# Routed expert rows scattered to both choices' places by the fused stage, and the two expert passes joined into one stream that adds into the output

## The chip, the cores and the metric

The kernel runs on one core of one Trainium2 chip. The metric is the time on the device in microseconds. Three runs of the kernel before gave 1041.34, 1044.93 and 1046.5 us; the median is 1044.93 us.

## The reference, cut to what matters

The input x has 32 batches of 256 tokens of 256 features (8192 tokens), float32. A gated cross-attention comes first; then every token goes through a shared gated MLP and through two of 16 experts:

```
x = x + tanh(g_xattn) * xattn(layernorm(x), ctx, ...)
xf = layernorm(x).reshape(-1, 256)
scores = softmax(xf @ Wg.T);  wk, idx = top_k(scores, 2)
cw = sum(one_hot(idx, 16) * wk)
h = gated_mlp_act(xf @ W1[e])                    # 256 -> 2*128 -> 128, for each expert
z = sum over e of cw[t, e] * (h @ W2[e])
x = x + tanh(g_ffn) * (z + gated_mlp_act(xf @ Ws1) @ Ws2)
```

The change touches only how the rows of the tokens reach their experts, and how the two experts' results are added.

## The kernel before

The kernel has four stages, one after the other: a preparation, the attention (batch by batch, until about 540 us of the profiled span), the fused stage `mix` (until about 752 us) and the expert stage `passes` (until the end).

**mix.** It goes through the 8192 tokens in 16 steps G of 512 tokens. A step holds its tokens in one of NX = 5 buffers `row[G % NX]`, 128 partitions x 4 x ROW with ROW = 516: columns 0 to 255 are the running sum (x1, to which the shared MLP's result is added), 256 to 511 the normalised token y, and the last four are the tail: the token's number, its place (slot) for the first choice, and the two weights. For each step TensorE transposes y, scores the experts, does the shared MLP (`hidden`, `down`) and counts places (`rank`); VectorE chooses the two experts (`choose`), writes the places (`place`, L1172) and the weights (`weigh`, L1159) and adds the MLP's result (`add_x1`, L1199, which counts up `added`). GpSimd's program for a step is: `note(G)` (the token numbers, L942), `low_weights(G)` (the low half of expert G's weights, L947, which waits for ScalarE's high half, L1073), then `scatter(G - 1)`: four indirect DMAs of 128 rows each (L956) that put whole 2064-byte rows into `rows1_scratch`, at the place for the second choice. SyncE loads the rows of step G + 3 (L887) when the scatter of step G - 2 has freed their buffer, and the weights; after the last step it writes blank rows behind each expert's last row (`blank_tails`, 16 DMAs, L1286).

**passes.** Each pass takes 80 tiles of 128 rows, which belong to one expert each, as 40 pairs. The first pass reads `rows1_scratch`, computes the second choice's expert, adds the result to the running sum in the row and scatters the whole 2064-byte row to the first choice's place in `rows0_scratch` (L1364). The second pass reads `rows0_scratch`, adds the first choice's expert and scatters 1024-byte rows to the output (L1364 again). For pair q:

- SyncE (`load`, L1335) waits until buffer `row[q % U]`, U = 10, has been scattered, loads two row numbers (L1341) and issues two DMAs (L1344).
- TensorE does `transpose_rows(q)` (L1386, 4 transposes), `hidden(q - 1)` (12 products into ps_h), `transpose_a(q - 2)` (L1407) and `down(q - 3)` (6 products into ps_z). These products are recorded under the lines of the helper `products`, L75 to L77.
- ScalarE copies the high halves (L1457, L1467) and does the silu (L1462); VectorE makes the low halves (L1482, L1495), multiplies (L1489), and adds ps_z to the row (L1500), which counts up `final`.
- GpSimd (`send`, L1359) waits for `final`, and issues two indirect DMAs.

After the loads of pair q == U SyncE writes all 16 blank tails of `rows0_scratch`. Between the passes it waits for every scatter of the first pass (L1352), since the second pass reads what they wrote. TensorE, ScalarE and VectorE run each pass as 10 written-out pairs, a hardware loop over three further rounds of 10, and a drain; GpSimd runs a loop over 4 rounds in each pass.

Of the kernel before, what the change touches and what calls it, by code (L numbers as in the profile page):

```python
# [28 lines left out]
P = 128  # L29
# [425 lines left out]
def attend(nc, c, a):  # L455


    with ExitStack() as ctx:
# [45 lines left out]
        with nc.Block() as block:  # L504

            @block.sync
            def _(sp):
# [6 lines left out]
                def blank_rows(dram):  # L514

                    sp.dma_start(dram[SLOT_ROWS:ROWS, :], c.blank[:, :]).then_inc(c.blanked, 16)
# [19 lines left out]
                blank_rows(c.rows1)  # L536
                blank_rows(c.rows0)
# [258 lines left out]
def mix(nc, c):  # L796
# [6 lines left out]
    with ExitStack() as ctx:  # L803
# [52 lines left out]
        l_done, masked, gap_ready, tanh_done = sem("l_done"), sem("masked"), sem("gap_ready"), sem("tanh_done2")  # L856
        ranked, counted, placed, chain = sem("ranked"), sem("counted"), sem("placed"), sem("chain")
# [15 lines left out]
        with nc.Block() as block:  # L873

            @block.sync
            def _(sp):
# [30 lines left out]
                blank_tails(nc, sp, nc.sync, c, c.rows1, 1, range(E), c.blanked1)  # L907

            @block.gpsimd
            def _(pool):  # L910
# [29 lines left out]
                def note(G):  # L940
                    wait(pool, scattered[G % NX], 64 * (G // NX))
                    g.tensor_copy(tail_of(G)[:, :, 0].bitcast(I32), tokens[:, 4 * G:4 * G + 4]).then_inc(noted, 1)  # L942
# [22 lines left out]
                for u in range(NX):  # L965
                    pool.wait_ge(scattered[u], 64 * len(range(u, STEPS, NX)))
# [147 lines left out]
            def _(v):  # L1114
# [44 lines left out]
                def weigh(G):  # L1159
# [10 lines left out]
                    V.tensor_tensor(tail[:, :, 3], over[:, :, E], tail[:, :, 2], ALU.mult)  # L1170

                def place(G):  # L1172
                    wait(v, scattered[G % NX], 64 * (G // NX))
# [103 lines left out]
def blank_tails(nc, eng, queue, c, dram, choice, experts, done):  # L1277


    for first in experts[::4]:  # L1280
        with ExitStack() as registers:
            held = [registers.enter_context(eng.register(f"tail_{choice}_{first + i}")) for i in range(4)]
            eng.load(held, c.tails[0:1, choice * E + first:choice * E + first + 4])
            for register in held:
                at = eng.snap(register, donate=True, min_val=0, max_val=SLOT_ROWS - P)
                queue.dma_start(dram[bass.ds(at, P), :], c.blank[:, :]).then_inc(done, 16)  # L1286


def passes(nc, c):


    U = 10
    ROUNDS = PAIRS // U
    YROW, META_AT = D, 2 * D
    with ExitStack() as ctx:
# [13 lines left out]
        go = sem("send_go")  # L1309
# [5 lines left out]
        def rounds(eng, step, first, lag=0):  # L1315


            last = first + ROUNDS
            for u in range(U):
                step(U * first + u, u, first)  # L1320
            with eng.Fori(first + 1, last) as j:
                for u in range(U):
                    step(U * j + u, u, j)
            for u in range(lag):
                step(U * last + u, u, last)

        def inside(first):

            return lambda q: not isinstance(q, int) or U * first <= q < U * (first + ROUNDS)

        with nc.Block() as block:

            @block.sync
            def _(sp):
                def load(dram, q):  # L1335
                    u = q % U
                    wait(sp, scattered[u], 32 * (q // U))
                    with ExitStack() as registers:
                        held = [registers.enter_context(sp.register(f"rows_{q}_{i}")) for i in range(2)]
                        first = 2 * q  # L1340
                        sp.load(held, c.rows_at[0:1, first:first + 2])  # L1341
# [9 lines left out]
                for u in range(U):  # L1351
                    sp.wait_ge(scattered[u], 32 * ROUNDS)  # L1352
                sp.wait_ge(c.blanked0, 16 * E)
                for q in range(PAIRS, 2 * PAIRS):
                    load(c.rows0, q)

            @block.gpsimd
            def _(pool):
                def send(q, u, dram, columns, index, bound):  # L1359
                    pool.wait_ge(final, q + 1)  # L1360
                    pool.sem_inc(go, 1)
                    for i in range(2):
                        target = row[u][:, i, META_AT + index:META_AT + index + 1].bitcast(I32)
# [4 lines left out]
                with pool.Fori(0, ROUNDS) as j:  # L1368
                    for u in range(U):
                        send(U * j + u, u, c.rows0, ROW, 1, SLOT_ROWS - 1)  # L1370
                with pool.Fori(ROUNDS, 2 * ROUNDS) as j:
                    for u in range(U):
                        send(U * j + u, u, c.out, D, 0, T - 1)
                for u in range(U):
                    pool.wait_ge(scattered[u], 64 * ROUNDS)

            @block.tensor
            def _(pe):


                def transpose_rows(q, u, j):
                    pe.wait_ge(row_in[u], 32 * (j + 1))
                    wait(pe, yT_lo, q - 1)
                    for i in range(2):
                        for k in range(DC):
                            last = nc.tensor.transpose(ps_y[u % 2][:, k, i * P:(i + 1) * P],  # L1386
                                                       row[u][:, i, YROW + k * P:YROW + (k + 1) * P], c.ident[:, :])
# [6 lines left out]
                def hidden(q, p, at):  # L1394
                    pe.wait_ge(yT_lo, q + 1)
                    wait(pe, a_done, 2 * (q - 1))
                    for i in range(2):
                        token = slice(i * P, (i + 1) * P)
                        last = products(nc, ps_h[p][:, i, :], [
                            (yT[p][0][:, k, token], yT[p][1][:, k, token], *split(at[i], k * D)) for k in range(DC)])  # L1400
                    last.then_inc(h_done, 1)

                def transpose_a(q, p):
                    pe.wait_ge(a_done, 2 * q + 2)
                    wait(pe, aT_lo, q - 1)
                    for i in range(2):
                        last = nc.tensor.transpose(ps_a[p][:, i, :], a[p][:, i, :], c.ident[:, :])  # L1407
                    last.then_inc(aT_done, 1)

                def down(q, p, at):  # L1410
                    pe.wait_ge(aT_lo, q + 1)
                    wait(pe, final, q - 1)
                    for i in range(2):
                        last = products(nc, ps_z[p][:, i, :], [
                            (aT[p][0][:, i, :], aT[p][1][:, i, :], *split(at[i], DC * D))])
                    last.then_inc(z_done, 1)

                def load_weights_at(known, q, u):


                    _, at = nc.values_load_multi_w_load_instructions(
                        c.weights_at[0:1, bass.ds(2 * q + 2, 4)], engines=[mybir.EngineType.PE], min_val=0,
                        max_val=(E - 1) * WROW, skip_runtime_bounds_check_because="the table is made of min(., E - 1)")
                    known[u], known[u + 1] = at[0:2], at[2:4]

                for first in (0, ROUNDS):
                    exists, known = inside(first), {}

                    def step(s, u, j):
                        if u == 0:  # L1430
                            known.clear()
                            if exists(s - 3):
                                load_weights_at(known, s - 3, -3)
                        if u % 2 == 0:
                            load_weights_at(known, s - 1, u - 1)
                        if exists(s):
                            transpose_rows(s, u, j)
# [148 lines left out]
```

## Time and profile before

| | us |
|---|---|
| median of the runs | 1044.93 |
| the profiled execution | 1043.86 |
| its span in the trace | 1041.7 |
| TensorE busy | 909.5 (87%) |
| VectorE busy | 804.5 (77%) |
| ScalarE busy | 478.8 (46%) |
| GpSimd busy | 475.1 (46%) |

All times below are from the start of this span. 2.2 us of the execution's own time lie outside it. Busy time is that of recorded instructions; an engine that waits, or issues DMAs, isn't counted as busy. PE is TensorE, PEld its weight loads, DVE VectorE, ACT ScalarE, POOL GpSimd, SPq and POOLq the sequencers of SyncE and GpSimd.

### The profile page before, as it was taken

To read this page: it belongs to the slowest core of one execution; us is meant where nothing else is said; L and a number is where in the kernel's file an instruction comes from. 1 tells how busy PE (TensorE), PEld (TensorE's weight loads), DVE (VectorE), ACT (ScalarE), POOL (GpSimd) and SP (SyncE) were. 2 spreads that over 40 slices of the span, in tenths; PEclk is the share of its full clock that TensorE was granted. 3 is DMA by queue.
4 is the path that set the end of the run, shared out by engine and by line. 5 is a ranking of instruction groups with operands and counts; after the bars stand their busy time and mean duration, and the time that the engine had idled before them with its cause. 6 is when DMAs were issued, how large, how long until landed. Compare 5 with 4: busy or idle time off the path is not lost. (4 is left out here: it accounts for less than half of the span.)

```text
span 1041.7 us, 22369 instructions
## 1 busy us (share of the span) xinstructions
PE 909.5 (87%) x6728; PEld 857.2 (82%) x6729; DVE 804.5 (77%) x1837; ACT 478.8 (46%) x970; POOL 475.1 (46%) x495
## 2 busy tenths in 40 slices
PE   2559999999999999999949999999565899599994
PEld 2449999999999999998847888887465899499994
DVE  5768888888898888998737898888534677467773
ACT  3345555555555555554445455543122344144441
POOL 6134434343343434334321555455415466537775
PEclk9999999999999999999968999999868899889998
DMA  8621222122221222212151444442769899488890
GB/s 216 215 87 35 80 68 67 54 57 79 66 79 45 66 66 67 68 54 67 53 172 32 173 166 160 170 170 108 275 222 318 284 341 344 146 267 260 268 289 29
DMA packets 108096, 150.64 MB, mean 145 GB/s; under 512 B 21622, under 2 KB 72186, under 8 KB 108032
## 3 DMA queue, kind: packets, MB, share of 16 engines
q1 hardware_dynamic: 92672, 107.60, 34.1%
q0 software_dynamic: 15360, 42.24, 10.6%
q8 instruction: 35, 0.57, 0.2%
q14 instruction: 29, 0.24, 0.1%
HBM read 90.19 MB, written 65.90 MB: 150 GB/s over the span
## 5 line engine op out<-in xcount | busy, mean ns | idle before, releaser
L549 POOL TENSOR_TENSOR prob<-prob,row_sum 128x616 f32<-128x616 f32 x64 | 77.9, 1218 | 148.7 <-DVE row_sum L739 148.7
L1364 POOL DMA_INDIRECT rows_scratch<-prow x80 | 78.7, 983 | 75.0 <-DVE prow L1500 47.2
L956 POOL DMA_INDIRECT rows_scratch<-row,slot x64 | 67.8, 1060 | 75.8 <-DVE row L1203 61.2
L1364 POOL DMA_INDIRECT out<-prow x80 | 78.7, 983 | 50.1 <-issue 26.4
L1482 DVE TENSOR_TENSOR eyT_lo<-ps_ey,eyT_hi 128x512 fp32r<-128x512 f32 x80 | 55.2, 690 | 55.6 <-ACT eyT_hi L1457 55.1
L1457 ACT ACTIVATE eyT_hi<-ps_ey 128x512 fp32r<-128x512 f32 x80 | 47.9, 599 | 109.3 <-PE ps_ey L1386 109.3
L75 PE MATMUL ps_h<-w_flat,eyT_hi 128*128 x320 | 98.1, 307 | 0.0
L224 POOL TENSOR_TENSOR xT_lo<-xT_raw,xT_hi 128x512 fp32r<-128x512 f32 x32 | 41.2, 1286 | 121.7 <-ACT ctxb_hi L190 121.6
L1386 PE MATMUL ps_ey<-ident,prow 128*128 128x128 f32 x320 | 51.6, 286 | 49.2 <-DMA prow<-rows_scratch 45.9
L190 ACT ACTIVATE M_hi<-ps_proj 128x308 f32 (+1 forms) x128 | 54.4, 429 | 84.1 <-PE ps_proj L77 84.0
L76 PE MATMUL ps_h<-w_flat,eyT_hi 128*128 x320 | 90.9, 284 | 0.0
L77 PE MATMUL ps_h<-w_flat,eyT_lo 128*128 x320 | 90.7, 283 | 0.0
L75 PE MATMUL ps_s<-M_hi,xT_hi 128*128 (+1 forms) x256 | 81.4, 318 | 8.7 <-PEq L315 8.5
L1489 DVE SCALAR_TENSOR_TENSOR a<-ps_h,prow,silu 128x128 f32<-128x128 f32 x160 | 48.8, 347 | 47.8 <-ACT silu L1462 47.8
L195 DVE TENSOR_TENSOR PT_lo<-ps_pt,PT_hi 77x512 fp32r<-77x512 f32 x128 | 80.9, 671 | 0.3 <-ACT PT_hi L190 0.3
L1386 PEld LDWEIGHTS ps_ey<-ident,prow 128*128 128x128 f32 x320 | 38.5, 147 | 51.7 <-DMA prow<-rows_scratch 47.3
L76 PE MATMUL ps_s<-M_lo,xT_hi 128*128 (+1 forms) x256 | 78.6, 307 | 0.0
L77 PE MATMUL ps_s<-M_hi,xT_lo 128*128 (+1 forms) x256 | 78.6, 307 | 0.0
L75 PE MATMUL ps_o<-wo_hi,OT_hi 128*128 128x256 f32 x256 | 74.6, 291 | 1.4 <-DVE OT_lo L195 1.4
L75 PE MATMUL ps_o<-PT_hi,V_hi 96*128 96x256 f32 x256 | 72.9, 285 | 3.3 <-DVE PT_lo L195 3.3
L675 ACT ACTIVATE prob<-prob,rstd 128x616 f32<-128x616 f32 x64 | 52.0, 812 | 44.8 <-DVE prob L729 44.8
L76 PE MATMUL ps_o<-PT_lo,V_hi 96*128 96x256 f32 x256 | 72.4, 283 | 0.0
(232 smaller groups left out, 3383.3 us busy)
## 6 DMA issues: line engine op xcount, KB each, us to landing
prow<-rows_scratch SPq DMA_DIRECT2D x160, 258.0 KB, 3.8
rows_scratch<-blank SPq DMA_DIRECT2D x34, 258.0 KB, 4.0
xs<-in_x SPq DMA_DIRECT2D x16, 512.0 KB, 4.5
xT_raw<-in_xT SPq DMA_DIRECT2D x32, 256.0 KB, 3.8
x_tok<-in_x SPq DMA_DIRECT2D x32, 256.0 KB, 2.9
x_scratch<-x_tok SPq DMA_DIRECT2D x32, 256.0 KB, 3.0
row<-x_scratch SPq DMA_DIRECT2D x16, 512.0 KB, 4.0
w_raw<-in_W SPq DMA_DIRECT2D x16, 256.0 KB, 3.5
```

The lines of the kernel that those rows point to most:

```text
L75: nc.tensor.matmul(out, lh, rh, start=start and n == 0, stop=False)
L76: nc.tensor.matmul(out, lh, rl, start=False, stop=False)
L77: last = nc.tensor.matmul(out, ll, rh, start=False, stop=stop and n == len(pairs) - 1)
L190: nc.scalar.activation(out, source, ACT.Copy).then_inc(done, 1)
L195: nc.vector.tensor_tensor(lo, source, f32(hi), ALU.subtract).then_inc(done, 1)
L549: nc.gpsimd.tensor_tensor(pr, pr, row_sum[i][:, :].unsqueeze(2).broadcast_to((P, H, CK)), ALU.mult).then_inc(normed, 1)
L675: nc.scalar.activation(prob[i][:, :], prob[i][:, :], ACT.Exp, scale=c.rstd1[:, bass.ds(2 * b + i, 1)]).then_inc(exp_done, 1)
L956: pool.indirect_dma_start(c.rows1, bass.IndirectOffsetOnAxis(slot1[:, t:t + 1], 0), row[G % NX][:, i, :], None).then_inc(scattered[G % NX] ...
L1364: pool.indirect_dma_start(dram, bass.IndirectOffsetOnAxis(target, 0), row[u][:, i, 0:columns], None, bounds_check=bound, oob_is_err=False) ...
L1386: last = nc.tensor.transpose(ps_y[u % 2][:, k, i * P:(i + 1) * P], row[u][:, i, YROW + k * P:YROW + (k + 1) * P], c.ident[:, :])
L1482: V.tensor_tensor(yT[p][1][:, :, :], ps_y[p][:, :, :], f32(yT[p][0][:, :, :]), ALU.subtract).then_inc(yT_lo, 1)
L1489: V.scalar_tensor_tensor(a[p][:, i, :], ps_h[p][:, i, 0:HID], row[b][:, i, weight:weight + 1], silu[p][:, i, :], ALU.mult, ALU.mult).then_ ...
```

## The change

The fused stage now scatters each row to both choices' places. `rows1_scratch` gets the whole row as before; `rows0_scratch` has rows of 260 floats (1040 bytes: y and the tail), and gets four further indirect DMAs for each step, issued ahead of the four old ones once `weigh` has counted up a new semaphore `weighed`. A buffer is free after 128 instead of 64 counts (each DMA counts 16).

In the expert stage the first pass scatters its 1024-byte sums to the output, and the second pass, which loads only 1040-byte rows, adds to the output with an indirect DMA that has `compute_op=add`. VectorE's last operation of a pair is a copy in the second pass instead of an addition. SyncE no longer waits between the passes; GpSimd waits there, once, until the first pass's scatters have landed. The blank tails of `rows0_scratch` are half as large and are written in four groups of four. U is 13 instead of 10, and all engines' programs are written out for 80 pairs, without loops. The core of the diff:

```diff
                 def load_rows(G):
                     u = G % NX
-                    wait(sp, scattered[u], 64 * (G // NX))
+                    wait(sp, scattered[u], 128 * (G // NX))
...
                 def scatter(G):
                     pool.wait_ge(noted, G + 1)
+                    pool.wait_ge(weighed, G + 1)
+                    for i in range(4):
+                        slot0 = row[G % NX][:, i, 2 * D + 1:2 * D + 2].bitcast(I32)
+                        pool.indirect_dma_start(c.rows0, bass.IndirectOffsetOnAxis(slot0, 0),
+                                                row[G % NX][:, i, D:], None).then_inc(scattered[G % NX], 16)
                     for i in range(4):
                         if i % 2 == 0:
                             pool.wait_ge(added, 2 * G + i // 2 + 1)
...
-                    V.tensor_tensor(tail[:, :, 3], over[:, :, E], tail[:, :, 2], ALU.mult)
+                    V.tensor_tensor(tail[:, :, 3], over[:, :, E], tail[:, :, 2], ALU.mult).then_inc(weighed, 1)
...
-    U = 10
-    ROUNDS = PAIRS // U
+    U = 13
+    LAST = 2 * PAIRS
...
                         for i in range(2):
                             at = sp.snap(held[i], donate=True, min_val=0, max_val=ROWS - P)
-                            sp.dma_start(row[u][:, i, :], dram[bass.ds(at, P), :]).then_inc(row_in[u], 16)
+                            if q < PAIRS:
+                                sp.dma_start(row[u][:, i, :], c.rows1[bass.ds(at, P), :]).then_inc(row_in[u], 16)
+                            else:
+                                sp.dma_start(row[u][:, i, D:], c.rows0[bass.ds(at, P), :]).then_inc(row_in[u], 16)
                 sp.wait_ge(c.blanked1, 16 * E)
                 for q in range(PAIRS):
-                    load(c.rows1, q)
-                    if q == U:
-                        blank_tails(nc, sp, nc.sync, c, c.rows0, 0, range(E), c.blanked0)
-                for u in range(U):
-                    sp.wait_ge(scattered[u], 32 * ROUNDS)
+                    load(q)
+                    first = (q - U) * 4 // 6
+                    if q >= U and (q - U) % 6 == 0 and first < E:
+                        blank_tails(nc, sp, nc.sync, c, c.rows0, 0, range(first, first + 4), c.blanked0, c.blank[:, D:])
                 sp.wait_ge(c.blanked0, 16 * E)
-                for q in range(PAIRS, 2 * PAIRS):
-                    load(c.rows0, q)
+                for q in range(PAIRS, LAST):
+                    load(q)
...
-                def send(q, u, dram, columns, index, bound):
+                def send(q, op):
                     pool.wait_ge(final, q + 1)
-                    pool.sem_inc(go, 1)
                     for i in range(2):
-                        target = row[u][:, i, META_AT + index:META_AT + index + 1].bitcast(I32)
+                        token = row[q % U][:, i, META_AT:META_AT + 1].bitcast(I32)
                         pool.indirect_dma_start(
-                            dram, bass.IndirectOffsetOnAxis(target, 0), row[u][:, i, 0:columns], None,
-                            bounds_check=bound, oob_is_err=False).then_inc(scattered[u], 16)
+                            c.out, bass.IndirectOffsetOnAxis(token, 0), row[q % U][:, i, 0:D], None, bounds_check=T - 1,
+                            oob_is_err=False, compute_op=op).then_inc(scattered[q % U], 16)
...
+                for q in range(PAIRS):
+                    send(q, ALU.bypass)
                 for u in range(U):
-                    pool.wait_ge(scattered[u], 64 * ROUNDS)
+                    pool.wait_ge(scattered[u], 32 * len(range(u, PAIRS, U)))
+                for q in range(PAIRS, LAST):
+                    send(q, ALU.add)
...
-                            V.tensor_tensor(row[b][:, :, 0:D], ps_z[p][:, :, :], row[b][:, :, 0:D],
+                        if q < PAIRS:
+                            V.tensor_tensor(row[q % U][:, :, 0:D], ps_z[q % 2][:, :, :], row[q % U][:, :, 0:D],
                                             ALU.add).then_inc(final, 1)
+                        else:
+                            V.tensor_copy(row[q % U][:, :, 0:D], ps_z[q % 2][:, :, :]).then_inc(final, 1)
```

## Rows read from the trace of the kernel before

**Rows 1.** Page, part 2: busy tenths in 40 slices of the span.
```profile
PE   2559999999999999999949999999565899599994
...
DMA  8621222122221222212151444442769899488890
```

**Rows 2.** Timeline of TensorE: start, us, instruction, idle before it.
```profile
764.20 1.11 PE L1386 MATMUL ps_ey<-ident,prow 128*128 128x128 f32 x4 [17.19 <-DMA prow<-rows_scratch]
...
810.46 1.12 PE L1386 MATMUL ps_ey<-ident,prow 128*128 128x128 f32 x4 [14.15 <-DMA prow<-rows_scratch]
...
837.75 0.63 PE L1386 MATMUL ps_ey<-ident,prow 128*128 128x128 f32 x4 [1.05 <-issue]
```

**Rows 3.** Stretches: us, busy by engine, clock, DMA share, GB/s.
```profile
577.00:697.00 120.00, 117.25 (x818) 102.94 (x817) 107.62 (x341) 60.98 (x123) 63.77 (x61) 1.00 0.47 167
...
840.00:895.00 55.00, 54.16 (x473) 53.99 (x473) 42.96 (x99) 24.43 (x59) 37.84 (x39) 1.00 0.94 328
...
925.00:1020.00 95.00, 94.57 (x825) 94.05 (x824) 74.96 (x172) 43.25 (x104) 67.52 (x69) 1.00 0.81 254
```

**Rows 4.** Timeline of VectorE: the last operation of a pair.
```profile
776.30 0.68 DVE L1500 TENSOR_TENSOR prow<-ps_z,prow 128x512 f32<-128x512 f32 x1
...
787.26 0.68 DVE L1500 TENSOR_TENSOR prow<-ps_z,prow 128x512 f32<-128x512 f32 x1
...
898.95 0.69 DVE L1500 TENSOR_TENSOR prow<-ps_z,prow 128x512 f32<-128x512 f32 x1 [0.35 <-PE ps_z L77]
...
923.35 0.68 DVE L1500 TENSOR_TENSOR prow<-ps_z,prow 128x512 f32<-128x512 f32 x1
...
1023.21 0.68 DVE L1500 TENSOR_TENSOR prow<-ps_z,prow 128x512 f32<-128x512 f32 x1
...
1027.74 0.69 DVE L1500 TENSOR_TENSOR prow<-ps_z,prow 128x512 f32<-128x512 f32 x1 [0.25 <-PE ps_z L77]
```

**Rows 5.** Line L956: time from its DMAs' issue to landing.
```profile
DMA to landing us min/median/max: 2.7/3.0/7.7
```

**Rows 6.** Timeline of SyncE's queue, 760 to 885 us.
```profile
760.70 23.33 SPq L1344 DMA_DIRECT2D prow<-rows_scratch  x22
784.54 17.83 SPq L1286 DMA_DIRECT2D rows_scratch<-blank  x16
```

**Rows 7.** Groups of GpSimd, 577.4 to 696.9 us (ten steps).
```profile
L956 POOL DMA_INDIRECT rows_scratch<-row,slot x40 | 43.2, 1080 | 47.6 <-DVE row L1203 38.5 <-issue 9.1
...
L942 POOL COPY row<-tokens 128x4 int32<-128x4 int32 x10 | 2.0, 203 | 0.0
```

**Rows 8.** Timeline of GpSimd in the fused stage.
```profile
565.18 1.84 POOL L947 TENSOR_TENSOR w_flat<-w_raw,w_flat 128x768 fp32r<-128x768 f32 x1 [14.57 <-ACT w_flat L1073]
...
637.20 1.85 POOL L947 TENSOR_TENSOR w_flat<-w_raw,w_flat 128x768 fp32r<-128x768 f32 x1 [0.82 <-ACT w_flat L1073]
...
646.75 1.38 POOL L956 DMA_INDIRECT rows_scratch<-row,slot  x1 [0.30 <-issue]
...
649.14 1.85 POOL L947 TENSOR_TENSOR w_flat<-w_raw,w_flat 128x768 fp32r<-128x768 f32 x1 [0.81 <-ACT w_flat L1073]
654.84 1.00 POOL L956 DMA_INDIRECT rows_scratch<-row,slot  x1 [3.85 <-DVE row L1203]
...
751.37 0.97 POOL L956 DMA_INDIRECT rows_scratch<-row,slot  x1 [0.30 <-issue]
```

**Rows 9.** Timeline of GpSimd at the end.
```profile
1024.76 0.98 POOL L1364 DMA_INDIRECT out<-prow  x1 [0.47 <-issue]
...
1033.78 0.98 POOL L1364 DMA_INDIRECT out<-prow  x1 [0.30 <-issue]
```

**Rows 10.** Page, part 3: DMA queues, packets, MB, share of 16 engines.
```profile
q1 hardware_dynamic: 92672, 107.60, 34.1%
q0 software_dynamic: 15360, 42.24, 10.6%
```

More of the change, by code:

```diff
@@ L906, in _ @@
                 sp.wait_ge(tails_ready, 1)
-                blank_tails(nc, sp, nc.sync, c, c.rows1, 1, range(E), c.blanked1)
+                blank_tails(nc, sp, nc.sync, c, c.rows1, 1, range(E), c.blanked1,
+                            c.blank[:, :])
             @block.gpsimd
@@ L965, in _ @@
                 for u in range(NX):
[L966 removed]
+                    pool.wait_ge(scattered[u], 128 * len(range(u, STEPS, NX)))
             @block.tensor
@@ L1274, in _, with blank_tails @@
                 V.tensor_copy(c.rows_at[:, :], ps_table[:, CHOICES * SLOT_TILES:])
-def blank_tails(nc, eng, queue, c, dram, choice, experts, done):
+def blank_tails(nc, eng, queue, c, dram, choice, experts, done, source):
     for first in experts[::4]:
         with ExitStack() as registers:
-            held = [registers.enter_context(eng.register(f"tail_{choice}_{first + i}")) for i in range(4)]
+            held = [registers.enter_context(eng.register(f"tail_{done.name}_{first + i}")) for i in range(4)]
             eng.load(held, c.tails[0:1, choice * E + first:choice * E + first + 4])
@@ L1313, in passes @@
             sem("aT_done"), sem("aT_hi"), sem("aT_lo"), sem("z_done"), sem("final"))
-        def rounds(eng, step, first, lag=0):
-            last = first + ROUNDS
-            for u in range(U):
[L1320 to L1329, printed above, removed]
         with nc.Block() as block:
@@ L1334, in _, with load @@
             def _(sp):
-                def load(dram, q):
+                def load(q):
                     u = q % U
@@ L1413, in down @@
                     for i in range(2):
-                        last = products(nc, ps_z[p][:, i, :], [
-                            (aT[p][0][:, i, :], aT[p][1][:, i, :], *split(at[i], DC * D))])
+                        last = products(nc, ps_z[q % 2][:, i, :], [
+                            (aT[q % 2][0][:, i, :], aT[q % 2][1][:, i, :], *split(at[i], DC * D))])
                     last.then_inc(z_done, 1)
[L1418 to L1437, printed above, removed]
-                        if exists(s - 1):
-                            hidden(s - 1, (u - 1) % 2, known[u - 1])
-                        if exists(s - 2):
-                            transpose_a(s - 2, u % 2)
-                        if exists(s - 3):
-                            down(s - 3, (u - 3) % 2, known[u - 3])
-                    rounds(pe, step, first, lag=3)
+                known = {}
@@ new lines, in _ @@
+                for s in range(LAST + 3):
+                    q = s - 1
+                    if 0 <= q < LAST and q % 2 == 0:
+                        registers = ExitStack()
+                        held = [registers.enter_context(pe.register(f"weights_{q}_{i}")) for i in range(4)]
+                        pe.load(held, c.weights_at[0:1, 2 * q + 2:2 * q + 6])
+                        at = [pe.snap(r, donate=True, min_val=0, max_val=(E - 1) * WROW) for r in held]
+                        known[q], known[q + 1] = (at[0:2], None), (at[2:4], registers)
+                    if s < LAST:
+                        transpose_rows(s)
+                    if 0 <= s - 1 < LAST:
+                        hidden(s - 1, known[s - 1][0])
+                    if 0 <= s - 2 < LAST:
+                        transpose_a(s - 2)
+                    if s >= 3:
+                        at, registers = known.pop(s - 3)
+                        down(s - 3, at)
+                        if registers:
+                            registers.close()
```

136 lines of the change are left out of this document (63 added, 73 removed).

## The prediction

> **What bounds the kernel now.** I read the busy slices first [rows 1]. TensorE is at nine tenths in most of the attention and the fused stage, and falls in three places of the last third, where the DMA row doesn't fall but mostly rises. The timeline of TensorE shows what two of them are [rows 2]: transposes of an expert pair that wait for loaded rows, 17.19 us ahead of the first pair and 14.15 us at 810. The third is the stop between the passes. Everywhere else the expert stage is bound by TensorE: from 840 to 895 us it is busy 54.16 of 55.00 us, from 925 to 1020 94.57 of 95.00, at a granted clock of 1.00, which is the 2.4 GHz level [rows 3]. A pair takes (787.26 - 776.30) / 4 = 2.74 us [rows 4]; over ten pairs it is 2.745, which I use. The fused stage is bound by TensorE too (117.25 of 120.00 us), while GpSimd has room: 63.77 of 120.00 [rows 3].
>
> **The expert stage.** From the first pair's last operation to the 80th's the trace has 1027.74 - 776.30 = 251.4 us [rows 4]. A stream at TensorE's pace takes 76 intervals of 2.745 us, 208.6 us, and for the last three, when no further pair is started, the 1027.74 - 1023.21 = 4.5 us seen now: 213.1 us. The difference of 38.3 us is what the change can take out here. It has three parts.
>
> - The stop between the passes: 923.35 - 898.95 = 24.4 us between two pairs [rows 4], in which the first pass drains, its scatters land and the loads begin anew. One interval of 2.7 us stays, and a pass that drains is quicker by 8.2 - 4.5 = 3.7 us, which the joined stream has once and not twice: 18.0 us go. Pass two no longer reads what pass one writes, so nothing on SyncE or TensorE waits there. The wait is GpSimd's alone, about 3 us from issue to landing [rows 5].
> - The stop at 810 with the slow matmuls behind it: SyncE spent 17.83 us on 16 blank DMAs between the loads of two pairs [rows 6], with ten buffers to live on. Now a group of four costs SyncE at most 4 x 17.83 / 16 = 4.5 us and writes half the bytes, and six pairs' loads (12 x 23.33 / 22 = 12.7 us) go with it: 17.2 us against six pairs of TensorE, 16.5 us. That is nearly even, and three more buffers give 8.2 us of distance. I cost the blanks at nothing; what hides them is that distance, and without it each group would cost its 4.5 us. About 17 us go.
> - The loops' ends: 1.05 us of idle TensorE at 837.75 [rows 2] and shorter ones at the other ends; the rest of the 38.3, about 3 us. Written-out code has no jump there. Should its code arrive late beside the busy DMA queues, at six places such a stop would cost 6 us; should it not, nothing. I take nothing, as 54.16 of 55.00 us hold one loop's end and no other stop.
>
> The DMAs have room. Pass one moved 328 GB/s at a share of 0.94; now it reads the same and writes half, which is what pass two does at present, at 254 GB/s and 0.81 [rows 3]. VectorE's last operation becomes a copy from the same PSUM tile, between nothing and its 0.68 us shorter; VectorE is busy 74.96 of 95 us and the path gets nothing of it. The weights' register loads are the same, one for two pairs.
>
> **The price in the fused stage.** GpSimd issues four more indirect DMAs for each of 16 steps. A group of four takes 4.32 us and 0.91 us of gaps now, 5.23 us [rows 7]; the four new ones, at 0.97 and 0.30 each, 5.1 us. The weights' low half is 1.85 us [rows 8], the copy 0.20 [rows 7], the gap behind them 0.3. That is 12.7 us of work for a step that now takes 649.14 - 637.20 = 11.94 us. GpSimd waits 3.85 us for `added` and 0.81 us for ScalarE's high half in it [rows 8], 4.7 us together, and these go first; what is over makes GpSimd this stage's bound. From its low_weights at 565.18 on it doesn't wait again: 567.0 + 0.3 + 16 x (5.23 + 5.10) + 14 x (0.20 + 1.85 + 0.30) = 765.5 us for its last scatter, instead of 751.37 + 0.97 = 752.3 [rows 8]. That is 13.2 us later. Queued behind the late scatters on GpSimd are `note` and `low_weights`, for which SyncE's loads of weights wait; for the scatters themselves SyncE's reload of the buffer waits, and for that ScalarE. Five buffers absorb the first steps' lateness, then TensorE gets small waits; these are the same lateness and don't add to it. The expert stage's first load waits for the last scatter, so all of it is on the path. The duration doesn't go by bytes: a 2064-byte row and a 1024-byte row give 0.97 and 0.98 us [rows 8, 9]. From both sides: if all 64 new ones were like the long one at 646.75, 1.38 us [rows 8], it would be 26 us more; if all new ones hid in the two waits, 13.2 less. I take the row that three of four show.
>
> **The adding DMA.** No row shows one. The nearest is the plain one: 0.98 us and a gap of 0.30, two for a pair, 2.56 us, 0.18 below TensorE's pair [rows 9]. A lower bound is the same 0.98 us (it must do all that the plain one does). For the upper one I count that an adding DMA moves a row three times (out of the buffer, out of the output, back) and a plain one twice: 0.98 x 3 / 2 = 1.47 us. At 0.98 pass two stays TensorE's, and GpSimd's wait of 3 us between the passes is made up in 17 pairs. GpSimd decides from (2.745 - 0.60) / 2 = 1.07 us on. Then from pair 40 it needs 3 us and 40 pairs of its own, where TensorE's pace ends after 36 x 2.745 + 4 x 2.56 = 109.1 us. At 1.47: 3 + 40 x 3.54 = 144.6, 35.5 us more. Rows of any kind cost GpSimd the same, so I stay near the plain row, a quarter of the way: 1.10 us, 3 + 40 x 2.80 = 115.0, 5.9 us more.
>
> The trace's indirect DMA takes 0.97 us for 128 rows of either length [rows 8, 9]. By the Trainium skill (Collectives: The Full Stack, "The bandwidth ceiling: the fold count and why AG ≠ RS ≠ AR") a reduce emits two read descriptors for each chunk where a copy emits one; if GpSimd's time went by descriptors, the sum would get the 35.5 us. By the same skill (DMA: Bandwidth & Descriptors, "Anatomy of one DMA") descriptor generation is a small part, and the sum would get nothing. No row here decides between them; the first is rival 2.
>
> The end is as before: 14.0 us from the last pair's operation to the span's end, in which GpSimd issues its last DMAs until 1034.8 [rows 4, 9].
>
> **The sum.** -38.3 + 13.2 + 5.9 = -19.2 us. From the profiled execution's own 1043.86 us that is 1024.7; it lay 1.1 us under the median of 1044.93, and against that I say 1025.7 us.
>
> **Rivals.**
>
> 1. Adding costs GpSimd nothing: -25.1 us, 1019.8. For it: the duration has no regard to bytes. Against: the second read must be described somewhere.
> 2. Adding costs GpSimd 1.47 us: -25.1 + 35.5 = +10.4, 1055, slower. It decides from 1.34 us on, where the gain is gone. For it: 128 rows in 0.98 us leave 8 ns for a row, which looks like work for each row. Pass two would have pairs of 3.54 us, ended by buffers that come free late.
> 3. The DMA engines can't add fast enough. The software queue moved 42.24 MB in 10.6% of 16 x 1041.7 us, 23.9 GB/s an engine, the hardware queue 18.9 [rows 10]. A pair of pass two loads 266 KB, 14.1 us of engine time, and adds 8192 / 40 rows of 1 KB, 8.8 us if plain; 16 engines have 43.9 us in a pair. The engines decide when an adding row costs 3.4 plain ones. At 4.5 a pair is 3.36 us: +24.5 us, 1044, the same. Against: 0.81 is the share now [rows 3].
> 4. GpSimd pays more in the fused stage, since it now always runs beside VectorE: 1 us more for a step, 16 us, 1041.7, the same. For it: the 1.38 us row; against: the other three of four.
> 5. The new scatters hide in GpSimd's idle half: -13.2, 1012.5. Against: its waits are 4.7 us of a step, its new work 5.1 and 0.3 more.
> 6. The blanks still starve TensorE, once by half of the old stop: +7, 1033. Against: 13 buffers.
>
> **The numbers.** Forecast, 1021.5 to 1034 with rival 6 in it: 0.42. Rival 1, 1018 to 1021.5: 0.22. Rival 5: 0.06. Rivals 3 and 4, 1034 to 1048: 0.17. Rival 2: 0.13. The likeliest cases' own range is 1018 to 1034. The range of 1013 to 1048 leaves out rival 2 and a part of rival 5, under 2 in 10. A measurement of this kernel can tell 0.5%, 5.2 us, from no change. Faster (below 1039.7): 0.42 + 0.22 + 0.06 and half of rivals 3 and 4, 0.78. Within 0.5%: 0.10, with the earliest of rival 2. Slower (above 1050.2): 0.12.
>
> **What would show it.** In the fused stage GpSimd almost without idle and steps of 12.7 us; its last scatter near 765; TensorE with small waits in the later steps. In the expert stage an unbroken row of nines, pairs of 2.745 us, and no wait of TensorE for rows except ahead of the first pair. GpSimd's adding DMA near 1.10 us. The prediction is wrong if that DMA is far above 1.1 us (pairs over 2.8 us, and finished pairs queued at the end), if transposes wait for rows in pass two while GpSimd waits too (slow adding), if the stream stops with the releaser "issue", or if the fused stage's steps stay at 11.95 us.

## The result: 1063.25 us, slower by 1.7%

The changed kernel took 1063.25 us in the median of four runs (1062.11 to 1064.02), the kernel before, beside it, 1045.11 us. The ratio is 1.0171 (95% interval 1.0148 to 1.0195). I had forecast 1025.7 us, a range of 1013 to 1048, and "slower" at 0.12: wrong in its direction, and outside the range.

The page of the changed kernel first: the busy slices, to be held against [rows 1], and one line of the groups.

```profile
PE   2659999999999999999849999998479999998840
...
POOL 5133434344443434344135888888616667788886
...
L1356 POOL DMA_INDIRECT out<-prow x160 | 203.6, 1273 | 85.6 <-issue 51.3
```

The three holes in TensorE's row have become one, as forecast. But its nines end early, and in the last slices, where TensorE has nothing to do, GpSimd goes on. Its 160 scatters of the expert stage have a mean of 1273 ns, and a mean over two forms hides both. GpSimd's timeline shows them: plain ones up to 902 us, the wait between the passes, then adding ones to the end.

```profile
902.18 0.99 POOL L1356 DMA_INDIRECT out<-prow  x1 [0.31 <-DMA out<-prow]
907.04 1.58 POOL L1356 DMA_INDIRECT out<-prow  x1 [3.88 <-DMA out<-prow]
908.93 1.59 POOL L1356 DMA_INDIRECT out<-prow  x1 [0.30 <-issue]
910.83 1.56 POOL L1356 DMA_INDIRECT out<-prow  x1 [0.30 <-issue]
...
1052.44 1.56 POOL L1356 DMA_INDIRECT out<-prow  x1 [0.30 <-issue]
1054.31 1.56 POOL L1356 DMA_INDIRECT out<-prow  x1 [0.30 <-issue]
```

An adding DMA takes 1.56 us and a gap of 0.30, so a pair costs GpSimd 3.72 us, and 40 pairs from 907.04 us on give 1055.8, where its last one ends. VectorE finished the last pair's rows long before. Its timeline shows the last operation of pairs 40 and 41, the first two of pass two when pairs are counted from 0, and of the last pair, 79:

```profile
902.22 0.68 DVE L1482 COPY prow<-ps_z 128x512 f32<-128x512 f32 x1
905.03 0.68 DVE L1482 COPY prow<-ps_z 128x512 f32<-128x512 f32 x1
...
1024.58 0.69 DVE L1482 COPY prow<-ps_z 128x512 f32<-128x512 f32 x1 [0.35 <-PE ps_z L77]
```

From its end at 1025.3 us on GpSimd works alone for 30.6 us, and the span ends 6.4 us later. How the lateness builds up stands in the windows (us, busy by engine PE, PEld, DVE, ACT, POOL with counts, clock, DMA share, GB/s):

```profile
577.00:697.00 120.00, 112.50 (x785) 98.84 (x783) 108.11 (x323) 59.88 (x119) 98.34 (x96) 1.00 0.56 198
840.00:895.00 55.00, 55.00 (x471) 54.94 (x470) 43.78 (x99) 24.50 (x58) 38.08 (x39) 1.00 0.81 257
900.00:920.00 20.00, 20.00 (x173) 20.00 (x172) 15.88 (x37) 8.91 (x22) 13.27 (x10) 1.00 0.57 98
920.00:940.00 20.00, 20.00 (x172) 19.97 (x172) 15.87 (x36) 8.80 (x21) 16.83 (x11) 1.00 0.82 138
940.00:1020.00 80.00, 68.07 (x545) 65.03 (x544) 50.20 (x115) 28.32 (x68) 66.89 (x44) 0.98 0.82 132
1040.00:1062.00 22.00, 0.00 (x0) 0.00 (x0) 0.00 (x0) 0.00 (x0) 13.43 (x9) 0.50 0.05 3
```

TensorE is full until 940 us, and by VectorE's timeline pairs go on at 2.81 us until 955: thirteen buffers and the rows already loaded let it run on at its own pace while unsent pairs pile up. Only then do the buffers run out, and it waits for rows whose load waits for GpSimd. GpSimd's 66.89 of 80 us is 44 x 1.56 minus the window's edges: the rest is the 0.30 us gap behind each, so it isn't idle at all. TensorE's small waits and the last 31 us are one and the same lateness. The waits of 795 to 1040 us name the rows, not their cause (us in total, times, longest):

```profile
POOL out L1356 <- issue: 47.8, 130, 0.6
...
PE ps_ey L1378 <- DMA prow<-rows_scratch: 11.7, 13, 2.7
```

The blanks starve nothing: TensorE waits 0.9 us for rows between its first transposes and 940 us. SyncE's queue (start, us spent issuing) answers to [rows 6]:

```profile
773.21 24.82 SPq L1336 DMA_DIRECT2D prow<-rows_scratch  x28
798.78 1.99 SPq L1295 DMA_DIRECT2D rows_scratch<-blank  x4
802.28 12.17 SPq L1336 DMA_DIRECT2D prow<-rows_scratch  x12
814.96 3.10 SPq L1295 DMA_DIRECT2D rows_scratch<-blank  x4
```

Between the two kernels' spans, 1041.7 and 1062.3 us, the 20.6 us divide so:

| stretch | before | after | difference |
|---|---|---|---|
| start to the expert stage's first load | 760.70 | 773.21 | +12.5 |
| to the first pair's last operation | 15.6 | 14.9 | -0.7 |
| to pair 40's (first of pass two) | 147.1 | 114.1 | -33.0 |
| to the end of the span | 118.3 | 160.1 | +41.7 |

### The profile page after: what moved, and what is told of

Read it like the earlier page. It is cut to its first block and busy times, and to the rows that moved or that the text cites. A ratio compares the mean times of both kernels' runs of the same rounds, so it can differ in the third digit from the quotient of the medians.

```text
span 1062.3 us, 21947 instructions
## 1 busy us (share of the span) xinstructions
PE 912.8 (86%) x6728; PEld 859.3 (81%) x6728; DVE 815.3 (77%) x1837; ACT 479.0 (45%) x970; POOL 583.6 (55%) x559
## 5 line engine op out<-in xcount | busy, mean ns | idle before, releaser
L1356 POOL DMA_INDIRECT out<-prow x160 | 203.6, 1273 | 85.6 <-issue 51.3
L965 POOL DMA_INDIRECT rows_scratch<-row,slot x64 | 67.5, 1055 | 19.5 <-issue 15.5
L77 PE MATMUL ps_o<-PT_hi,V_lo 96*128 96x256 f32 x256 | 73.0, 285 | 0.0
L959 POOL DMA_INDIRECT rows_scratch<-row x64 | 62.8, 981 | 17.5 <-issue 17.5
```

The costliest lines, as they stand in the source:

```text
L77: last = nc.tensor.matmul(out, ll, rh, start=False, stop=stop and n == len(pairs) - 1)
L959: pool.indirect_dma_start(c.rows0, bass.IndirectOffsetOnAxis(slot0, 0), row[G % NX][:, i, D:], None).then_inc(scattered[G % NX], 16)
L965: pool.indirect_dma_start(c.rows1, bass.IndirectOffsetOnAxis(slot1[:, t:t + 1], 0), row[G % NX][:, i, :], None).then_inc(scattered[G % NX] ...
L1356: pool.indirect_dma_start(c.out, bass.IndirectOffsetOnAxis(token, 0), row[q % U][:, i, 0:D], None, bounds_check=T - 1, oob_is_err=False, c ...
```

## The experiments

Thirteen runs follow, of eleven kernels. Each kernel is an edit of the changed one, but for two that edit the kernel before. A ratio is to the kernel before as it ran beside the kernel of the experiment, on the same chip; its median was 1043.71 or 1044.35 us.

**The second pass without adding.**

```diff
                 for q in range(PAIRS, LAST):
-                    send(q, ALU.add)
+                    send(q, ALU.bypass)
```

> The changed kernel, but the second pass's scatter writes instead of adding (the output then holds only the first choice's part). Theory A: the adding DMA's 1.56 us on GpSimd is all that makes pass two slow. Then each of its DMAs takes 0.98 us, pairs are 2.81 us as in pass one, and the execution loses about 41 us: near 1022. Rival: pass two would be slow anyway, from the doubled use of the output or from loads of 1040-byte rows; then pairs stay above 2.9 us and the time above 1030.

It took 1019.88 us (1018.76 to 1023.0), 0.9775 of the kernel before (0.974 to 0.981). Rival 1 had said 1019.8. All 160 scatters are alike now, and GpSimd's idle time is back (its groups from 785 us on):

```profile
L1356 POOL DMA_INDIRECT out<-prow x160 | 157.4, 984 | 90.0 <-issue 60.8 <-DVE prow L1479 24.5 <-DVE prow L1482 2.4
```

Behind the first pair TensorE waits for rows nowhere in the stream. The word "add" alone costs 1063.25 - 1019.88 = 43.4 us between the two medians. The two did not run side by side; by their ratios to the kernel before it is 1.0171 - 0.9775, some 41 us, and from pair 40 to the end of the span the traces have 160.1 us with it and 1019.2 - 899.2 = 120.0 without. So it is 40 to 43 us. With its measured 1.56 us my own formula gives 3 + 40 x 3.72 - 109.1 = 42.7. Everything else in the change is worth 24 us of gain, where the prediction had 25.1.

**Without the new scatters of the fused stage.** The second pass reads the columns y and tail of the first pass's rows; the waits go back to 64 counts.

```diff
-                    for i in range(4):
-                        slot0 = row[G % NX][:, i, 2 * D + 1:2 * D + 2].bitcast(I32)
-                        pool.indirect_dma_start(c.rows0, bass.IndirectOffsetOnAxis(slot0, 0),
-                                                row[G % NX][:, i, D:], None).then_inc(scattered[G % NX], 16)
...
-                                sp.dma_start(row[u][:, i, D:], c.rows0[bass.ds(at, P), :]).then_inc(row_in[u], 16)
+                                sp.dma_start(row[u][:, i, D:], c.rows1[bass.ds(at, P), D:]).then_inc(row_in[u], 16)
```

> The changed kernel, but the fused stage scatters only to rows1 (four DMAs for each step), and pass two reads the y and tail columns of rows1 at pass one's places, so that its values are wrong while its amount of work is the same. Theory A: the four further DMAs make the fused stage end later by their lateness on GpSimd, 13 to 14 us, and nothing else: near 1050, with the expert stage as in the changed kernel. Rival: they are hidden, and the later start comes from elsewhere: 1060 or more.

It took 1053.08 us (1049.29 to 1054.14), 10.2 less than the changed kernel; its first load comes at 759.90 instead of 773.21 us, 13.3 earlier. Of these 13.3 us, 4.5 were there before the fused stage's new scatters began (GpSimd's low weights just ahead of them start at 563.89 and 568.42 us), which leaves 8.8. GpSimd has its idle time of the fused stage again, as in [rows 7] (577 to 697 us):

```profile
L961 POOL DMA_INDIRECT rows_scratch<-row,slot x40 | 43.2, 1081 | 47.9 <-DVE row L1208 38.8 <-issue 9.1
```

So the step of the prediction that put the new scatters on the path holds, at 9 to 10 us instead of its 13.2. The price of adding outweighs the gain by itself: this kernel adds and has no new scatters, and is still slower than the kernel before (1.0093; 1.0064 to 1.0123). The price of the new scatters alone doesn't: the kernel of the experiment above pays it and is faster.

**Fewer rows for each scatter.** The passes' scatters send 64 or 16 of the 128 rows of a tile.

```diff
-                        token = row[q % U][:, i, META_AT:META_AT + 1].bitcast(I32)
+                        token = row[q % U][0:64, i, META_AT:META_AT + 1].bitcast(I32)
...
-                            c.out, bass.IndirectOffsetOnAxis(token, 0), row[q % U][:, i, 0:D], None, bounds_check=T - 1,
+                            c.out, bass.IndirectOffsetOnAxis(token, 0), row[q % U][0:64, i, 0:D], None, bounds_check=T - 1,
```

> The changed kernel, but both passes' indirect DMAs send only the first 64 of each tile's 128 rows (half of the output is missing). Theory A: GpSimd's time goes by the descriptions it writes, two for a plain row and three for an adding one. Then both durations fall, by rows: the plain one from 0.98 to 0.5 to 0.75 us, the adding one from 1.56 to 0.8 to 1.1, and the step between them halves from 0.58 to about 0.29 us. Rival B, a dearer fixed set-up for an adding DMA: the step stays at 0.58. Rival C, GpSimd is held back by the DMA engines that add: the adding one falls to the plain one's duration, since the engines then have half the work.

> The changed kernel, but both passes' indirect DMAs send only the first 16 of each tile's 128 rows (most of the output is missing). With 64 rows the durations were 0.91 and 1.41 us, with 128 they are 0.98 and 1.56. Theory B, a fixed set-up, dearer for an adding DMA, and a small part for each row: along that line 0.86 and 1.29 us. Theory A, all of it for rows, is left only if the durations now fall far below 0.8 and 1.2.

One run each: 1050.65 us with 64 rows, 1035.15 us with 16. With 64 rows, one plain DMA of GpSimd's timeline and the group of the second pass (915 to 1000 us); then the groups of both passes with 16 (870 to 895 and 915 to 985 us):

```profile
879.48 0.91 POOL L1356 DMA_INDIRECT out<-prow  x1 [0.30 <-issue]
...
L1356 POOL DMA_INDIRECT out<-prow x50 | 70.1, 1402 | 15.2 <-issue 13.4 <-DVE prow L1482 1.8
```

```profile
L1356 POOL DMA_INDIRECT out<-prow x19 | 16.0, 841 | 10.5 <-DVE prow L1479 7.4 <-issue 3.0
...
L1356 POOL DMA_INDIRECT out<-prow x45 | 57.5, 1278 | 13.7 <-issue 12.2 <-DVE prow L1482 1.5
```

| rows | plain, us | adding, us | difference |
|---|---|---|---|
| 16 | 0.84 | 1.28 | 0.44 |
| 64 | 0.91 | 1.40 | 0.49 |
| 128 | 0.98 | 1.56 | 0.58 |

A line through each column: plain 0.82 us and 1.3 ns for a row, adding 1.24 us and 2.5 ns. Of the 0.58 us, 0.42 is there however few rows are sent, and 0.16 goes by rows. A theory in which adding merely doubles the work for each row explains the second part, not the first. Why the fixed part is dearer no run shows. Even with 16 rows an adding DMA and its gap take 1.28 + 0.30 = 1.58 us, above the 2.745 / 2 = 1.37 us at which GpSimd begins to decide.

**A quarter of the bytes.** The scatters send 64 of the 256 columns.

```diff
-                            c.out, bass.IndirectOffsetOnAxis(token, 0), row[q % U][:, i, 0:D], None, bounds_check=T - 1,
+                            c.out.rearrange("t (k d) -> (t k) d", d=64), bass.IndirectOffsetOnAxis(token, 0), row[q % U][:, i, 0:64], None, bounds_check=T - 1,
```

> The changed kernel, but both passes' indirect DMAs send only the first 64 of a row's 256 columns, to rows of 256 bytes (most of the output is missing). Theory: GpSimd's time has nothing to do with bytes; the durations stay at 0.98 and 1.56 us, the pairs of pass two at 3.72 us and the time at about 1063. Rival: the adding DMAs are slow at the DMA engines and hold GpSimd back; then the 1.56 falls to 1.2 or less with a quarter of the bytes.

This kernel ran once, on a chip on which the kernel before took 1106.27 us, so its own 1109.86 us can't be set against the others; the duration on GpSimd can. All 160 together, and the last ones by the timeline:

```profile
L1356 POOL DMA_INDIRECT out<-prow x160 | 203.5, 1272 | 119.3 <-DVE prow L1479 74.3
```

```profile
1098.33 1.56 POOL L1356 DMA_INDIRECT out<-prow  x1 [0.30 <-issue]
1100.19 1.56 POOL L1356 DMA_INDIRECT out<-prow  x1 [0.30 <-issue]
```

The mean is within 1 ns of that with four times the bytes. Together with the run of 16 rows, where an eighth of the rows still takes 1.28 of the 1.56 us, it says that the cost is GpSimd's in issuing, not the transfer's, and rival 3 (the DMA engines) has nothing left to stand on.

**The blanks of the kernel before, moved.** Two kernels with the old design. In the first the 16 blank tails of `rows0_scratch` are issued at the end of the fused stage, in the second behind the first pass's last load.

```diff
                 blank_tails(nc, sp, nc.sync, c, c.rows1, 1, range(E), c.blanked1)
+                blank_tails(nc, sp, nc.sync, c, c.rows0, 0, range(E), c.blanked0)
```

```diff
                     load(c.rows1, q)
-                    if q == U:
-                        blank_tails(nc, sp, nc.sync, c, c.rows0, 0, range(E), c.blanked0)
+                blank_tails(nc, sp, nc.sync, c, c.rows0, 0, range(E), c.blanked0)
```

> The kernel before, but SyncE writes the blank tails of rows0 at the end of the fused stage, where it waits, instead of between the loads of pass one. If the stop at 810 us came from these 16 DMAs alone, it goes: 14 to 17 us less, near 1029. If the ring of ten buffers is too short for DMA queues at 0.94 of their time, part of it stays as waits for rows: 1035 to 1040.

> The kernel before, but SyncE writes the 16 blank tails of rows0 after the last load of pass one, where its queue waits for the drain. They are then beside scatters alone and must land before the wait for the last scatter is over. If so, the stop at 810 goes and the expert stage's start stays where it was: 15 to 17 us less, 1028 to 1030. If the blanks are still in flight at the pass's end, the stop between the passes grows by up to 6 us: 1034.

The early ones gave 1034.2 us (1031.65 to 1034.63), a ratio of 0.9901 (0.987 to 0.9932); the late ones 1030.09 us (1026.38 to 1032.89), 0.9873 (0.9836 to 0.9911). Both lose the stop at 810 us. The late ones came out as expected, the early ones 5 us slower than hoped: there the blanks delay the first load instead, from 760.70 to 768.08 us (SyncE's queue):

```profile
735.47 27.71 SPq L1287 DMA_DIRECT2D rows_scratch<-blank  x32
768.08 30.94 SPq L1345 DMA_DIRECT2D prow<-rows_scratch  x26
```

Late, they lie in the stop between the passes, which is there anyway, while the first pass drains (SyncE's queue until 960 us):

```profile
867.61 17.99 SPq L1286 DMA_DIRECT2D rows_scratch<-blank  x16
891.54 68.73 SPq L1344 DMA_DIRECT2D prow<-rows_scratch  x54
```

That is a gain of 14 us for one call moved out of a loop, behind its end. Of the kernels here that compute the whole, it is the fastest: below the kernel before and below the changed one.

**The joined stream without an adding DMA.** The first pass scatters its sums by the first choice's place into a scratch of their own, and the second loads them with SyncE, four pairs ahead, and adds on VectorE; eleven buffers.

```diff
+                def load_sums(q):
+                    u = q % U
...
+                            sp.dma_start(row[u][:, i, 0:D], c.sums0[bass.ds(at, P), :]).then_inc(sum_in[q % 4], 16)
...
+                for q in range(PAIRS, LAST):
+                    if q >= PAIRS + 4:
+                        sp.wait_ge(final, q - 3)
+                    load_sums(q)
+                    if q + 7 < LAST:
+                        load(q + 7)
```

> A joined stream without an adding DMA: the fused stage scatters as in the changed kernel; pass one writes its sums with the plain indirect DMA to a scratch by the first choice's places; pass two loads y and the tail early and the sums by a DMA of SyncE's, four pairs ahead of their use, once pass one's scatters have landed; VectorE adds them as before. 11 buffers. GpSimd then has 2.56 us for a pair in both passes. Between the passes VectorE's last operation waits for the first sums, some 5 to 9 us instead of a stop of 18. Expected 1022 to 1030: the 1020 of the writing second pass and that wait. Rival: the third and fourth load of a pair on SyncE's queue, or the DMA engines, make pass two slower than 2.81 us: 1035 or more.

1055.54 us (1053.71 to 1057.12), a ratio of 1.0106 (1.0082 to 1.0129): a miss, by the rival that was named. GpSimd is relieved, and the wait sits on VectorE (its groups, 905 to 1050 us, and SyncE's queue at 940 us):

```profile
L1498 DVE TENSOR_TENSOR prow<-ps_z,prow 128x512 f32<-128x512 f32 x41 | 28.3, 690 | 50.4 <-DMA prow<-sums_scratch 47.6 <-PE ps_z L77 2.3 <-issue 0.4
```

```profile
940.51 0.87 SPq L1355 DMA_DIRECT2D prow<-sums_scratch  x2
942.11 1.09 SPq L1340 DMA_DIRECT2D prow<-rows_scratch  x2
943.90 0.85 SPq L1355 DMA_DIRECT2D prow<-sums_scratch  x2
```

Two DMAs take SyncE mostly 0.85 us, but with the two row numbers for them a group starts only every 1.5 to 1.8 us, and a pair has two such groups: 3.1 to 3.6 us, over the 2.8 us that a pair takes where TensorE decides. From its first load of sums at 910.55 to 1050 us SyncE waits only once, for 0.2 us. The queue that was relieved at the boundary became the bound. From pair 40 to the last pair it takes 127.7 us, the kernel without adding 105.9: 22 us more. Up to pair 40 it takes 12.5 us more, at the boundary for the most part, where I had expected 5 to 9.

**Ten buffers.** Pairs in the changed kernel take 2.81 us, not 2.745. Theory: the written-out code. Rival: the thirteen buffers.

```diff
-    U = 13
+    U = 10
...
-                    send(q, ALU.add)
+                    send(q, ALU.bypass)
```

> The changed kernel with ten buffers instead of 13, and a writing instead of an adding second scatter (the output then holds only the first choice's part). Pairs take 2.81 us in the changed kernel's pass one and 2.74 before. Theory: written-out code costs it; then pairs stay at 2.81. Rival: the 13 buffers moved the other tiles in memory, or the deeper ring does it: then 2.74, and some 5 us less than with 13. If ten buffers are too few for four blanks between loads, TensorE shows waits for rows, some us in all.

One run, 1016.57 us. The last operations of its first pairs:

```profile
787.75 0.68 DVE L1479 TENSOR_TENSOR prow<-ps_z,prow 128x512 f32<-128x512 f32 x1
...
790.50 0.68 DVE L1479 TENSOR_TENSOR prow<-ps_z,prow 128x512 f32<-128x512 f32 x1
...
793.24 0.68 DVE L1479 TENSOR_TENSOR prow<-ps_z,prow 128x512 f32<-128x512 f32 x1
```

2.745 us again, in written-out code; the code isn't it. The buffers make the difference, by their number or by where the tiles behind them come to lie. I tried to tell these apart with a pad of 32 bytes behind thirteen and behind ten buffers, each kernel run twice.

```diff
         row = [sb(f"prow{i}", [P, 2, ROW]) for i in range(U)]
+        sb("pad", [P, 8])
```

> As e1 (13 buffers, a writing second scatter, the output holds only the first choice's part), with 32 unused bytes in each partition behind the buffers. 13 buffers of 4128 bytes end 32 bytes off a multiple of 64, 11 do too (pairs of 2.80 us), 10 don't (2.745). Theory: the tiles behind them lie badly for TensorE's reads, and with the 32 bytes pairs take 2.745 us again, 5 us less than e1 in all. Rival: the number of buffers itself does it; pairs stay at 2.81.

> As e5 (ten buffers, a writing second scatter, the output holds only the first choice's part), with the 32 unused bytes behind the buffers, which move the tiles behind them off the multiple of 64. Theory: pairs of 2.81 us instead of 2.745, about 5 us more than e5's 1016.6. Rival: no change.

> e9 again: 13 buffers with 32 unused bytes behind them, a writing second scatter. Theory of the tiles' place: pairs of 2.745 us, the time near 1015. Rival, the number of buffers: 2.81 us, 1020.

> e12 again: ten buffers with 32 unused bytes behind them, a writing second scatter. Theory of the tiles' place: pairs of 2.81 us. Rival: 2.745 us.

The four ran on two chips on which the kernel before takes 1106.27 and 1104.79 us: 1110.28 and 1118.23 us with thirteen, 1102.67 and 1116.42 with ten. There pairs of 2.1 and 5 us alternate in either kernel, which buries a difference of 0.065 us in the times of pairs.

Within a pair the traces say a little more. Most of the extra time, 0.05 to 0.06 of the 0.065 us, lies in the twelve products of `hidden`, which TensorE starts one after the other. Their second and their twelfth, with ten buffers, and with ten buffers and the pad (TensorE's timelines):

```profile
852.55 0.28 PE L76 MATMUL ps_h<-w_flat,eyT_hi 128*128 x1
...
853.70 0.28 PE L77 MATMUL ps_h<-w_flat,eyT_lo 128*128 x1
```

```profile
854.17 0.29 PE L76 MATMUL ps_h<-w_flat,eyT_hi 128*128 x1
...
855.36 0.28 PE L77 MATMUL ps_h<-w_flat,eyT_lo 128*128 x1
```

| kernel | pairs in the traces | 1.13 to 1.16 us | 1.17 to 1.20 us |
|---|---|---|---|
| ten buffers | 75 | 61 | 14 |
| ten, with the pad | 97 | 0 | 85 |
| thirteen, a writing second scatter | 75 | 0 | 75 |
| thirteen, on the slower chip (quarter of the bytes) | 52 | 0 | 48 |
| thirteen, with the pad | 96 | 8 | 78 |

The table counts pairs by the time between these two starts, until 1000 us, where all twelve products are in the trace; the pairs that are in neither column took longer. The kernels with the pad are taken together over both their runs. Thirteen buffers have the same pace on both kinds of chip. With ten, 32 bytes are enough for the slow pace, so the number of buffers isn't needed for it, though no run without the pad was made on those chips. But the same 32 bytes don't bring the fast pace back with thirteen, so my theory of the multiples of 64 doesn't hold as it stands. The cause of the 2.81 us stays open.

## Why the prediction was wrong, step by step

- **The stops of the expert stage: right in kind, 6.2 us too much.** Up to pair 40 the stream gained 33.0 us. The stop between the passes is gone: the last operations of pairs 40 and 41 start at 902.22 and 905.03, an interval like all others. The blanks stopped nothing; a group costs SyncE 2 to 3 us instead of my 4.5. The loops' ends gave nothing back in the sum, since pairs of 2.81 instead of 2.745 us ate it: in the kernel without adding the 79 intervals take 1005.05 - 785.73 = 219.3 us, where I had 213.1. The term of -38.3 us was mis-sized by these 6.2; it measured 32.1. VectorE's timeline of that kernel, the last operation of its first and last pair:

```profile
785.73 0.68 DVE L1479 TENSOR_TENSOR prow<-ps_z,prow 128x512 f32<-128x512 f32 x1
...
1005.05 0.69 DVE L1482 COPY prow<-ps_z 128x512 f32<-128x512 f32 x1 [0.20 <-PE ps_z L77]
```

- **The price in the fused stage: the mechanism right, 2 to 4 us too much.** Forecast: last scatter at 765.5 us, steps of 12.7. Measured, by GpSimd's timeline: 765.67 + 0.96 = 766.6, and 12.5.

```profile
568.42 1.84 POOL L949 TENSOR_TENSOR w_flat<-w_raw,w_flat 128x768 fp32r<-128x768 f32 x1 [13.00 <-ACT w_flat L1082]
...
693.87 1.85 POOL L949 TENSOR_TENSOR w_flat<-w_raw,w_flat 128x768 fp32r<-128x768 f32 x1
706.37 1.85 POOL L949 TENSOR_TENSOR w_flat<-w_raw,w_flat 128x768 fp32r<-128x768 f32 x1
...
765.67 0.96 POOL L965 DMA_INDIRECT rows_scratch<-row,slot  x1 [0.30 <-issue]
```

  That the two ends agree to 1.1 us is partly luck. This run's stage began 3.2 us later than that of the kernel before (568.42 instead of 565.18). From there to the last scatter's end it took 198.2 us, the kernel before 187.2: 11.0 us more, not 13.2. To the expert stage's first load it is 204.8 against 195.5, 9.3 us more.
- **The adding DMA: this step failed.** I took 1.10 us, "a quarter of the way" from 0.98 to 1.47, since "rows of any kind cost GpSimd the same". It is 1.56 us, outside my bounds too. The +5.9 became 40 to 43, and this alone turns -19.2 into about +18. Two errors are in it. The price went with the kind of operation, which none of my rows varied: rows of 2064 and 1024 bytes both belong to plain DMAs, so their equality says nothing on adding. And the upper bound counted rows moved, 3 for 2, which has nothing to do with what GpSimd spends: by the lines above 0.82 us of a plain DMA don't go by rows, and adding makes that 1.24.
- **Nearness taken for likelihood.** The forecast sat 0.03 us above the point where GpSimd decides (1.07), and 80 DMAs in a row stood behind it, so that 0.1 us was worth 8 us. Below that point nothing could be won, above it every tenth cost 8 us, so all of the uncertainty lay on one side. At such a place the chance of the upper case can't be 0.13 without a row for it.
- **Rival 2** had the mechanism and the direction: pairs of 3.7 us (3.54 there), finished pairs queued on GpSimd, buffers that come free late, 1055 us. It was short by 0.09 us a DMA, 7 us in 80 DMAs. Its reason was half right: it took 8 ns a row for work by rows, where the runs show 1.3 ns and a large fixed part. The Trainium skill (Collectives: The Full Stack, "The bandwidth ceiling: the fold count and why AG ≠ RS ≠ AR") has a reduce emit two read descriptors for each chunk, where a copy emits one. The part that goes by rows grows as they do, 2.5 for 1.3 ns, but no run here counts descriptors, and the fixed 0.42 us does not come out of it. By the Trainium skill (DMA: Bandwidth & Descriptors, "Anatomy of one DMA") making the descriptors is a small, variable part of a DMA. The part that goes by rows is small here too, 0.16 of 0.98 us for 128 plain rows; but GpSimd's whole time for the instruction, 1.56 us when it adds, set the pace of a pass.
- **Rivals 4 and 5** fell. The new scatters have a mean of 981 ns over all 64 and the old ones 1055, where the kernel before has 1060, so nothing was stretched; and 9.3 us of them arrived at the first load, so they were not hidden. Rival 6 fell with the blanks, rival 3 with the quarter of the bytes. Rival 1 gave the time of the kernel without adding to 0.1 us, and that closeness is luck: the expert stage gained 6.2 us less than I had and the fused stage cost 2 to 4 us less, which partly cancel, and against the kernel before beside it (1043.71 us) the gain was 23.8 us, not 25.1.

## What to carry to other kernels

Before work is moved onto a queue that has 0.2 us to spare in each turn, price it in the form it will have there; a row of the same instruction without the option that is new is no price, and a bound must come from what the engine does, not from what the transfer does. Where a one-sided threshold is that near, weigh the far end heavily, since a small error is multiplied by every turn behind it. And look first for the cheap part of a large change: one call moved out of a loop gave 14 us, where the whole rebuilding lost 18.

## What the runs showed of the hardware

An indirect DMA from GpSimd took 0.84, 0.91 and 0.98 us for 16, 64 and 128 rows, and an adding one 1.28, 1.40 and 1.56 us, each with 0.30 us behind it; at 128 rows it was the same for rows of 256 and 1024 bytes. In the kernel that loads its sums SyncE needed about 1.6 us for two row numbers and the two DMAs that use them, 0.85 us of it for the DMAs. A stage whose tiles and products are the same took 2.745 us for a pair with ten row buffers and 2.81 with thirteen. From the second to the twelfth product of `hidden` it is 1.13 to 1.16 us in most pairs with ten and 1.19 to 1.20 with thirteen, and 1.17 to 1.20 in most pairs with ten and 32 unused bytes behind them; why is open.
